# Layer 0 of a four-layer kernel: the experts' products are taken of the unweighted input, and VectorE weighs them out of PSUM between its recurrence steps; GpSimd's part goes

## What is computed

```python
# s: complex linear recurrence over 256 steps in each of 4 sequences
xh = x @ W_in + b_in
gate_x = sigmoid(block_diag(xh, W_gx)); gate_a = sigmoid(block_diag(xh, W_ga))
a = exp(complex(-8*gate_a*softplus(a_real), a_imag*gate_a))
xc = sqrt(1 - a**2) * complex(*split(xh, 2)) * gate_x
h = linear_scan(a, xc)                  # h[t] = a[t]*h[t-1] + xc[t]
s = concat(h.real, h.imag) @ W_out + b_out

# f: 8 experts, the top 2 of each token, and a shared expert
shared = silu(x @ shared_gate_w) * (x @ shared_up_w) @ shared_down_w
probs  = top-2 mask * sigmoid(x @ router_w)
xin  = probs.T[:, :, None] * x[None]
gu   = einsum('etd,edf->etf', xin, gate_up_w)
gate, up = split(gu, 2)
f = shared + einsum('eti,eid->etd', silu(gate) * up, down_w).sum(0)
```

## Time and profile before

| | |
|---|---|
| median of 3 runs | 1097.79 us (1097.26 to 1098.12) |
| the profiled execution, whole | 1094.99 us |
| its span in the profile | 1093.1 us |
| TensorE's granted clock, mean | 0.978 of full |
| TensorE / VectorE / ScalarE / GpSimd busy | 93% / 67% / 45% / 35% |
| layer 0's stage behind its norm | about 16 to 163 us of the span |
| its expert loop on TensorE | 56.9 to 148.6 us |

### The profile page before, as it was taken

One profiled execution on the slowest core, in us unless ns is written; L12 is line 12 of the kernel. 1 busy time (PEld: TensorE's weight loads), 2 busy tenths in 40 slices (PEclk: granted clock), 3 DMA queues, 4 the chain that ended last, 5 costly groups with the idle time before them and its releaser, 6 DMA issues. The chain is left out here.

```text
span 1093.1 us, 13859 instructions
## 1 busy us (share of the span) xinstructions
PE 1011.5 (93%) x4720; PEld 615.9 (56%) x4720; DVE 728.6 (67%) x1070; ACT 494.9 (45%) x1048; POOL 380.8 (35%) x285
## 2 busy tenths in 40 slices
PE   6999988997999999998998888987999989999997
PEld 4455564633566566565564555564666767555554
DVE  2689974435999999884927666775666631756652
ACT  3543223446988788522214445553666631111112
POOL 0198920005888788821003233200544520000000
PEclk8999999999999999998999899998999999999999
DMA  4112205004000000008215344220000000010001
GB/s 123 40 59 71 72 0 179 1 2 116 18 22 20 21 30 10 1 1 238 78 39 131 89 104 104 43 83 18 1 1 1 1 1 29 29 58 30 29 0 38
DMA packets 53920, 52.85 MB, mean 48 GB/s; under 512 B 9832, under 2 KB 48840, under 8 KB 53856
## 3 DMA queue, kind: packets, MB, share of 16 engines
q1 hardware_dynamic: 50256, 47.31, 14.5%
q0 software_dynamic: 3072, 4.20, 2.4%
q10 hardware_dynamic: 528, 0.52, 0.1%
HBM read 44.45 MB, written 5.47 MB: 46 GB/s over the span
## 5 line engine op out<-in xcount | busy, mean ns | idle before, releaser
L1035 POOL TENSOR_TENSOR seen<-state,c_row 128x512 f32<-128x512 f32 x128 | 160.7, 1277 | 38.5 <-PE banks L1173 27.6
L1055 DVE TENSOR_TENSOR_SCAN state<-decay,banks 128x512 f32<-128x512 f32 x128 | 155.5, 1217 | 19.5 <-ACT decay L1004 8.2
L2401 PE MATMUL banks<-xnT,weight 128*128 128x512 f32 x256 | 115.0, 592 | 1.0 <-PEq L2128 1.0
L2135 POOL TENSOR_TENSOR prob<-prob,inverse 128x512 f32<-128x512 f32 x64 | 65.3, 1041 | 113.4 <-DVE inverse L2220 113.4
L994 ACT ACTIVATE weighed_x<-dx_tok,b_tok 128x512 f32<-128x512 f32 x128 | 90.5, 712 | 24.9 <-PE banks L1159 23.3
L1159 PEld LDWEIGHTS banks<-ident,weighed_x 128*128 128x128 f32 x512 | 59.4, 142 | 60.9 <-ACT weighed_x L994 38.4
L1004 ACT ACTIVATE decay<-delta_pairs,A 128x510 f32<-128x510 f32 x128 | 90.9, 710 | 6.2 <-DVE state L1055 6.2
L2442 DVE TENSOR_TENSOR inter<-gelu,banks 128x512 f32<-128x512 f32 x32 | 22.0, 688 | 96.7 <-ACT gelu L2433 96.0
L204 PE MATMUL banks<-ident 128*128 128x512 f32 x156 | 75.4, 622 | 11.4 <-PEq L2480 8.7
L1159 PE MATMUL banks<-ident,weighed_x 128*128 128x128 f32 x512 | 80.8, 282 | 3.7 <-DVE state L1055 3.2
L2433 ACT ACTIVATE gelu<-banks 128x512 f32<-128x512 f32 x32 | 19.1, 598 | 138.1 <-PE banks L2401 138.1
(11 more groups left out here) (370 smaller groups left out, 1945.1 us busy)
## 6 DMA issues: line engine op xcount, KB each, us to landing
prob_row<-probs_dram SPq DMA_DIRECT2D x8, 512.0 KB, 4.1
c_row<-c_dram SPq DMA_DIRECT2D x32, 128.0 KB, 2.9
slot_wide_w<-in_L_ffn_w_gate SPq DMA_DIRECT2D x16, 176.0 KB, 2.4
slot_wide_w<-in_L_ffn_w_up SPq DMA_DIRECT2D x16, 176.0 KB, 2.6
slot_down_w<-in_L_ffn_w_down SPq DMA_DIRECT2D x16, 176.0 KB
gate_up_w<-in_L_ffn_gate_up_w SPq DMA_DIRECT2D x8, 256.0 KB, 4.2
delta_pairs<-conv_in SPq DMA_DIRECT2D x8, 256.0 KB, 3.5
w_WqT<-in_L_attn_W_q SPq DMA_DIRECT2D x1, 2048.0 KB, 9.7
```

The source lines that it names most:

```text
L1035: nc.gpsimd.tensor_tensor(seen[:, u % ring, :], state[:, u % ring, :], c_row[:, v % 4, :], ALU.mult).then_inc(seen_ready, 1)
L1055: nc.vector.tensor_tensor_scan(state[:, u % ring, :], decay[:, u % ring, :, :].rearrange("p b t -> p (b t)"), banks[:, 4 + u % 2, :], 0.0, ...
L2135: nc.gpsimd.tensor_tensor(prob[:, u % 2, h, :, :], prob[:, u % 2, h, :, :], inverse[:, u % 2, h, :].unsqueeze(2).broadcast_to([P, 2, SEQ]) ...
L2401: last = nc.tensor.matmul(banks[:, 4 + 2 * half + j, :], weight[:, s, j, k, tile * P:(tile + 1) * P], xnT[:, k, cols[half]], start=(k == 0 ...
```

## The change

- Raises read `xnT` itself. VectorE multiplies both products by the probability row as it takes them out of PSUM: `weigh(n)` writes `gate_in` and `up` (512 wide, two operations). ScalarE then takes the silu of `gate_in` from SBUF, and VectorE makes `expert_hT` (`hidden(n)`). ScalarE's copies of the up bank go.
- For the shared expert, ScalarE takes silu from PSUM, and VectorE multiplies it by the up bank (`shared`).
- These VectorE operations are written into the recurrence's list, one `hidden` and one `weigh` every two or three recurrence operations. GpSimd has only its two memsets of `inside` left in the stage; `x_in` goes.
- The recurrence is reordered a little: `gate_x` multiplies xh (two products) rather than the two coefficients, the negation of zi is folded into a constant, and the reciprocal is cut into two halves.
- TensorE turns the probabilities between the two gates' products and not after them, and ScalarE copies them between its gate sigmoids. The six dummy products ahead of the loop go.
- SyncE asks for the probability row after the gate and up weights, behind VectorE's `emptied`.

```diff
-        x_in = m.sbuf("expert_x", [P, 2, KD, N])
+        gate_in = m.sbuf("expert_gate", [P, 2, HALF])
...
-                        sp.wait_ge(x_in_ready, 4 * i + 2 * s - 2)
-                        load_prob(2 * i + s, s)
                         sp.wait_ge(raised, 4 * i + 2 * s)
                         load_gate_up(2 * i + s, s)
+                        sp.wait_ge(emptied, 4 * i + 2 * s)
+                        load_prob(2 * i + s, s)
...
-                def raise_(half, wide, x, count=None):
+                def raise_(half, wide, count=None):
 
                     if count is not None:
-                        pe.wait_ge(evacuated, count)
+                        pe.wait_ge(emptied, count)
                     for j in range(2):
                         for k in range(KD):
-                            last = nc.tensor.matmul(banks[:, 4 + 2 * half + j, :], wide(j, k), x(k)[:, cols[half]],
+                            last = nc.tensor.matmul(banks[:, 4 + 2 * half + j, :], wide(j, k), xnT[:, k, cols[half]],
...
-                        pe.wait_ge(x_in_ready, job + 1)
-                        raise_(half, lambda j, k: gate_up_w[:, s, k, j * width:(j + 1) * width],
-                               lambda k: x_in[:, s, k, :], 2 * job + 2)
+                        raise_(half, lambda j, k: gate_up_w[:, s, k, j * width:(j + 1) * width], job + 1)
...
-                pe.wait_ge(probs_ready, 1)
-                for t in range(NT):
-                    last = nc.tensor.transpose(banks[0:experts, t // 4, (t % 4) * P:(t % 4 + 1) * P],
-                                               probs[:, t, :], ident[:, :])
-                last.then_inc(probs_turned, 1)
+                    if gate == 0:
+                        pe.wait_ge(probs_ready, 1)
+                        for t in range(NT):
+                            last = nc.tensor.transpose(banks[0:experts, t // 4, (t % 4) * P:(t % 4 + 1) * P],
+                                                       probs[:, t, :], ident[:, :])
+                        last.then_inc(probs_turned, 1)
...
-                keep_busy(nc, banks[:, 3, :], ident, 6)
...
-                def evacuate(job, half, count=None):
-
-                    act.wait_ge(raised, job + 1)
-                    if count is not None:
-                        act.wait_ge(ffn_h_ready, count)
-                    nc.scalar.activation(silu[:, half, :], banks[:, 4 + 2 * half, :], ACT.Silu).then_inc(evacuated, 1)
-                    nc.scalar.activation(up[:, half, :], banks[:, 5 + 2 * half, :], ACT.Identity).then_inc(evacuated, 1)
+                def shared(half):
+
+                    act.wait_ge(raised, half + 1)
+                    nc.scalar.activation(silu[:, half, :], banks[:, 4 + 2 * half, :], ACT.Silu).then_inc(silu_ready, 1)
 
                 def expert(e):
                     for half in range(2):
-                        evacuate(2 * e + 2 + half, half, 2 * e + 1 + half)
+                        act.wait_ge(gate_in_ready, 2 * e + half + 1)
+                        act.wait_ge(ffn_h_ready, 2 * e + half + 1)
+                        nc.scalar.activation(silu[:, half, :], gate_in[:, half, :], ACT.Silu).then_inc(silu_ready, 1)
...
-                def weigh(i, s, first=False):
-
-                    pool.wait_ge(prob_loaded[s], DMA * (i + 1))
-                    for half in range(2):
-                        if not first:
-                            pool.wait_ge(raised, 4 * i + 2 * s + half - 1)
-                        nc.gpsimd.tensor_tensor(
-                            x_in[:, s, :, cols[half]], xnT[:, :, cols[half]],
-                            prob[:, s, cols[half]].unsqueeze(1).broadcast_to([P, KD, HALF]), ALU.mult
-                            ).then_inc(x_in_ready, 1)
...
-                def hidden(job, half, count=None):
-
-                    pool.wait_ge(evacuated, 2 * job + 2)
-                    if count is not None:
-                        pool.wait_ge(lowered, count)
-                    nc.gpsimd.tensor_tensor(ffn_hT[:, half, :], silu[:, half, :], up[:, half, :], ALU.mult
-                                            ).then_inc(ffn_h_ready, 1)
...
+                def shared(half):
+
+                    dve.wait_ge(silu_ready, half + 1)
+                    dve.wait_ge(raised, half + 1)
+                    nc.vector.tensor_tensor(ffn_hT[:, half, :], silu[:, half, :], banks[:, 5 + 2 * half, :], ALU.mult
+                                            ).then_inc(ffn_h_ready, 1)
+                    dve.wait_ge(ffn_h_ready, half + 1)
+                    dve.sem_inc(emptied, 1)
+
+                def weigh(n):
+
+                    e, half = n // 2, n % 2
+                    dve.wait_ge(raised, n + 3)
+                    dve.wait_ge(prob_loaded[e % 2], DMA * (e // 2 + 1))
+                    nc.vector.tensor_tensor(gate_in[:, half, :], banks[:, 4 + 2 * half, :], prob[:, e % 2, cols[half]], ALU.mult
+                                            ).then_inc(gate_in_ready, 1)
+                    nc.vector.tensor_tensor(up[:, half, :], banks[:, 5 + 2 * half, :], prob[:, e % 2, cols[half]], ALU.mult
+                                            ).then_inc(emptied, 1)
+
+                def hidden(n):
+                    half = n % 2
+                    dve.wait_ge(emptied, n + 3)
+                    dve.wait_ge(silu_ready, n + 3)
+                    dve.wait_ge(lowered, n + 1)
+                    nc.vector.tensor_tensor(ffn_hT[:, half, :], silu[:, half, :], up[:, half, :], ALU.mult
+                                            ).then_inc(ffn_h_ready, 1)
 
...
+                    if q >= 2:
+                        shared(q - 2)
+
+                dve.wait_ge(gate_x_ready, 2)
+                both(xh[:, 0, :], xh[:, 0, :], ALU.mult, gate_x[:, :])
+                both(xh[:, 1, :], xh[:, 1, :], ALU.mult, gate_x[:, :])
+                weigh(0)
                 dve.wait_ge(waves_ready, 2)
                 dve.wait_ge(radius_ready, 2)
                 both(ta[:, :], radius2[:, :], ALU.mult, wave[:, 0, :])
-                both(tb[:, :], radius2[:, :], ALU.mult, wave[:, 1, :])
+                both(zi[:, :], radius2[:, :], ALU.mult, wave[:, 1, :])
                 steps.add(nc.vector.memset(radius[:, starts], 0.0))
                 steps.join()
+                hidden(0)
+                weigh(1)
                 steps.add(nc.vector.tensor_scalar(zr[:, :], ta[:, :], -1.0, 1.0, ALU.mult, ALU.add))
-                steps.add(nc.vector.tensor_scalar(zi[:, :], tb[:, :], -1.0, None, ALU.mult))
-                steps.join()
-                both(ta[:, :], zr[:, :], ALU.mult, zr[:, :])
                 both(tb[:, :], zi[:, :], ALU.mult, zi[:, :])
                 steps.join()
+                steps.do(nc.vector.tensor_tensor(ta[:, :], zr[:, :], zr[:, :], ALU.mult))
                 nc.vector.tensor_tensor(ta[:, :], ta[:, :], tb[:, :], ALU.add).then_inc(square_ready, 1)
+                hidden(1)
+                weigh(2)
                 dve.wait_ge(modulus_ready, 1)
                 steps.do(nc.vector.tensor_tensor(tb[:, :], tc[:, :], zr[:, :], ALU.add))
 
                 nc.vector.tensor_scalar(ta[:, :], tb[:, :], 0.5, 1e-30, ALU.mult, ALU.max).then_inc(square_ready, 1)
+                hidden(2)
+                weigh(3)
                 dve.wait_ge(modulus_ready, 2)
-                steps.do(nc.vector.reciprocal(tb[:, :], tc[:, :]))
-                steps.do(nc.vector.scalar_tensor_tensor(td[:, :], zi[:, :], 0.5, tb[:, :], ALU.mult, ALU.mult))
-
-                dve.wait_ge(gate_x_ready, 2)
-                both(tc[:, :], tc[:, :], ALU.mult, gate_x[:, :])
-                both(td[:, :], td[:, :], ALU.mult, gate_x[:, :])
-                steps.join()
+                steps.do(nc.vector.reciprocal(tb[:, cols[0]], tc[:, cols[0]]))
+                hidden(3)
+                weigh(4)
+                steps.do(nc.vector.reciprocal(tb[:, cols[1]], tc[:, cols[1]]))
+                hidden(4)
+                weigh(5)
                 both(ta[:, :], tc[:, :], ALU.mult, xh[:, 0, :])
+                both(radius2[:, :], tc[:, :], ALU.mult, xh[:, 1, :])
+                steps.do(nc.vector.scalar_tensor_tensor(td[:, :], zi[:, :], -0.5, tb[:, :], ALU.mult, ALU.mult))
+                hidden(5)
+                weigh(6)
                 both(tb[:, :], td[:, :], ALU.mult, xh[:, 1, :])
-                both(radius2[:, :], tc[:, :], ALU.mult, xh[:, 1, :])
                 both(turns[:, :], td[:, :], ALU.mult, xh[:, 0, :])
                 steps.join()
                 both(zr[:, :], ta[:, :], ALU.subtract, tb[:, :])
+                hidden(6)
+                weigh(7)
                 both(zi[:, :], radius2[:, :], ALU.add, turns[:, :])
                 steps.join()
 
@@ -625,24 +628,38 @@
                 cos, sin = wave[:, 2, :], wave[:, 3, :]
                 both(ta[:, :], zr[:, :], ALU.mult, cos)
                 both(tb[:, :], zi[:, :], ALU.mult, sin)
+                hidden(7)
+                weigh(8)
```

(60 more changed lines are left out.)

2 lines of the change are left out of this document (1 added, 1 removed).

## The result

The changed kernel takes 1081.62 us (median of four runs, 1079.67 to 1085.24) against 1097.53 us in the same comparison; the ratio is 0.9865, 95% interval 0.9832 to 0.9899. That is 15.9 us, where I had forecast 10.3 and at most 12.

What follows compares the result with a forecast made beforehand. TensorE sets the expert loop's beat, with VectorE and GpSimd nearly full. 5.4 us from the earlier start plus 4.9 of 5.7 lost in the loop give 10.3: 1097.8 - 10.3 = 1087.5 us, range 1085.0 to 1092.5.

Steps and rivals of the forecast that it cites:

- TensorE's floor: Expert loop: sixteen half-jobs of 5.16 us plus two last lowers, 86.0 us if VectorE never makes TensorE wait.
- R0: First raise of the expert loop: forecast to start at about 51.5 us where 56.9 stood, 5.4 us earlier.
- VectorE's prices: VectorE operation costs without GpSimd: 1024-wide product 1.13 or 1.25 us, scan 2.29, half reciprocal 3.3, hidden 0.62, weigh product 0.66.
- The allowance of 0.8 us for queued waits: VectorE's recurrence: 0.02 to 0.03 us added for each of some 35 operations with extra waits queued in front.
- GpSimd as what stretches VectorE: Expert loop: GpSimd's reads lengthen VectorE's 1024-wide products of two SBUF tensors, from 1.22 to 3.41 us.
- Cost nothing themselves: Six dummy products ahead of the loop, 5.3 us: they lay in a wait, so removing them was priced at nothing.
- The loop of the kernel before: Expert loop, 56.9 to 148.6 us: 91.7 us, of which 5.7 lost to waits; 4.9 of these to be saved.
- Nothing ahead of the loop changes: Part ahead of the changed code: kept as in the one trace, with only 5.4 us taken off the first raise.
- (a): VectorE's queued waits make it the bound: 0.1 us more per operation gives 1090.3 us, 0.2 gives 1093.8; chance 0.22.
- (b): VectorE's long operations come from TensorE, ScalarE or DMA traffic, not GpSimd: slower, 1122 us; chance 0.05.
- (c): Clock falls because TensorE idles from 49.9 to 51.5 without dummies: half clock for 8 us costs 4, 1091.5 us; chance 0.04.
- (d): Change does nothing, since TensorE stays the bound and loses only dummies; inside the 0.05 chance of "within 0.2%".

Runs made afterwards that it cites:

- gpsimd_reads: Changed kernel plus 24 unused 1024-column GpSimd products with both operands in SBUF, from the first weigh on: 1117.85 us, ratio 1.0193.
- gpsimd_writes: Changed kernel plus 70 GpSimd memsets of 1024 columns, which read nothing and write SBUF: 1080.4 us.
- dummies_back: Changed kernel with the six dummy products back ahead of the loop: 1085.37 us.
- before_again: Kernel before, run and profiled again with nothing edited: median 1094.9 us over 12 runs, ratio to itself 0.9991.

## Why the prediction missed, point by point

*TensorE's floor: right.* 86.0 us from R0 on; measured 86.09, 86.09, 86.08 and 86.09 in four profiles.

*VectorE's prices: right but for PSUM.* 1.13, 1.25, 2.29 and 3.3 us came as priced, and the wait for the second root is 2.47 us where I had 2.4. `weigh` steps by 0.60 where I took 0.66 from the scalar forms: 32 products, 1.9 us too much, 1.6 of it in the thirteen slots to hidden(12). The overhead for PSUM in the Trainium skill (Perfetto Trace Analysis, Optimizing Scalar/DVE Operations) would have given slightly more still; this trace does not agree with it for such products, whose step is the same as from SBUF. hidden(12) ends 73.3 us behind R0 and not 74.5, so VectorE's slack is 2.4 us and not 1.2. (For hidden(11) I wrote 122.1; by my own terms it is 126.0 - 2.4 - 1.9 = 121.7, a little early and not late.) The allowance of 0.8 us for queued waits came on top of that sum, and nothing of it is there. Of all this only the allowance changed the time.

*GpSimd as what stretches VectorE: right, though one row was misread.* I wrote that both short products fall into GpSimd's gap. The second one runs from 93.95 to 95.17, and GpSimd multiplies from 93.98. It had started 0.03 us earlier, and it was not stretched. The argument stands on `gpsimd_reads` and `gpsimd_writes`, not on those rows.

*R0: right, against its own stage.* It stands 8.7 us behind the first shared product; forecast 51.5 - 42.9 = 8.6. "Cost nothing themselves" holds for the dummies only while R0 waits for `expert_x`; my 5.4 us counted R0 as free of them, and `dummies_back` shows that 3.3 us of it hang on their going.

*The loop of the kernel before: mis-sized.* I took 91.7 us from one execution. Five give 91.7, 92.9, 92.5, 92.1 and 92.8, mean 92.4: 0.7 us more to be saved. The difference lies in longer waits for GpSimd and in the low clock behind the longest of them (2.49 to 2.56 us, in three of the five). From the first shared product to the output product the stage takes 106.4 us before on the mean and 94.8 after: 11.6 us.

*Nothing ahead of the loop changes: the step that failed.* I kept the early part of the one trace as it stood and took only 5.4 us off R0, from 56.9 to 51.5. R0 came at 46.82. In the pair of profiles this step carried 4.8 us (42.91 against 38.13). In all runs the difference of medians is 1096.0 - 1081.1 = 14.9 us; at equal mean clock (0.980, by a line through each kernel's runs) it is 1093.9 - 1082.4 = 11.5, close to the stage's 11.6. The remaining 3.4 us go with the mean clock. An early low stretch costs 4.8 us, and three of five profiles of the kernel before have it: 2.9 us on the mean. The match is rough, because the clock costs time behind the stage as well: from the output product to the end of the span the five profiles of the kernel before take 944.3 to 951.4 us, mean 948.0, and the four of the changed kernel 944.7 to 949.5, mean 946.3. These 1.7 us are less than the scatter of either kernel. So how the 3.4 us divide between the early stretch and the rest is an estimate, and the cause of the early low clock stays open. I had read that stretch and used it only to price a fall of the clock in the changed kernel. That it might be absent there was in none of my cases. The one trace that I worked from has the loss; with `before_again` as that trace, R0 would have been forecast 4.8 us earlier. Why no profile of the changed kernel has it, nothing here shows.

*The range: too narrow for that reason.* I set it by a "run to run spread under 1 us", from three runs. The spread of this kernel is 14.7 us (1088.5 to 1103.2).

*The rivals.* (a) fell: no wait costs anything on VectorE; its price was right in kind, since work beyond the slack goes one to one into the end. (b) fell: `gpsimd_writes` and the 1.22 us rows show it. `gpsimd_reads` shows the kind of damage; that its 1118 us lie near the 1122 of (b) is chance, since I chose how many products GpSimd got. (c) fell: the granted clock is 1.00 from R0 to the output product, behind an idle stretch of 1.67 us. (d) fell: TensorE stayed the bound, and what it gained was its waits and the earlier R0.

## What to carry to other kernels

Two engines whose SBUF reads hold each other up cost twice: moving some 30 us of work onto a VectorE that seemed 91% full made the stage shorter, since about 31 of its 83 busy microseconds were stretching by GpSimd's weigh products. So before a busy engine is called full, compare the same operation with and without its neighbour at work. And before one execution is taken as the kernel before, ask which of its stretches ran at a low clock, and whether all executions do: here that was worth as much as a third of the change.

## What the runs showed of the hardware

- Beside GpSimd products that read SBUF, most of VectorE's two-operand SBUF products are stretched, up to 3.40 us from 1.22, and a scalar form from 0.69 to 2.76; a product with one PSUM operand keeps 0.68, and GpSimd's memsets disturb none.
- 512-wide f32 products step by 0.60 us on VectorE, from PSUM as from SBUF.
- With waits of TensorE of 2.49 to 2.56 us in the old loop (four profiles) the granted clock went to 0.50 for some 3 us; with waits of 1.66 to 1.87 us, in the old loop and ahead of the new one, it stayed at 1.00.
- Executions of one program differ by up to 14.7 us (the runs are from several chips), most of it in step with the mean granted clock (0.9 us for 0.001).
